# The second cross attention of a two-layer decoder follows one written table instead of rules by step

## What is computed

```python
q = x @ w_q + b_q                  # x: 2048 x 256
k = context @ w_k + b_k            # context: 1601 x 192
v = context @ w_v + b_v
q, k, v = (t.reshape(B, -1, 16, 16) for t in (q, k, v))      # 16 heads of 16
weights = softmax(einsum('bqhd,bkhd->bhqk', q, k) / 4, axis=-1)
out = einsum('bhqk,bkhd->bqhd', weights, v).reshape(B, Lq, 256)
x = layernorm(x + out @ w_o + b_o)
```

## Time and profile before

| | us |
|---|---|
| median of three executions (lowest, highest) | 3368.96 (3361.8, 3370.19) |
| the profiled execution's own time | 3361.29 |
| its span on the core | 3359.5 |
| first scores of unit 0 to the last values of unit 15 | 2530.6 to 3154.1 |

### The profile page before, as it was taken

The page is one execution under the profiler, slowest core; times in us unless marked ns, Lnnn a source line. Parts: engine busy times, 40 slices in busy tenths (PEclk is TensorE's granted clock), DMA queues, the critical chain, the costliest instruction groups (busy, mean ns, idle before and its releaser), DMA issues. The chain is left out here.

```text
span 3359.5 us, 62575 instructions
## 1 busy us (share of the span) xinstructions
PE 3055.7 (91%) x24201; PEld 1779.1 (53%) x24201; DVE 2373.0 (71%) x4987; ACT 1697.8 (51%) x2102; POOL 1735.9 (52%) x1163
## 2 busy tenths in 40 slices
PE   7999999989999999999999827779989999999797
PEld 3666666654555555555555406646654434444346
DVE  5999999945676666776667382175448979888418
ACT  3888888843444444444444322222325756666641
POOL 5999999924878788787888802223440000000002
PEclk9999999989999999999999958979988999999898
DMA  2000000020000000000000076610021201210101
GB/s 69 9 2 2 2 2 2 27 55 3 4 1 4 1 4 4 1 4 1 4 1 1 1 236 195 168 41 1 1 45 18 28 9 23 28 21 2 34 1 38
DMA packets 65530, 91.51 MB, mean 27 GB/s; under 512 B 9586, under 2 KB 55539, under 8 KB 64371
## 3 DMA queue, kind: packets, MB, share of 16 engines
q1 hardware_dynamic: 61682, 83.17, 9.8%
q0 software_dynamic: 3072, 4.34, 0.7%
q10 hardware_dynamic: 512, 0.26, 0.0%
HBM read 62.34 MB, written 10.65 MB: 22 GB/s over the span
## 5 line engine op out<-in xcount | busy, mean ns | idle before, releaser
L980 DVE TENSOR_REDUCE x0hm<-x0pM 128x1 f32<-128x400 f32 (+1 forms) x1024 | 536.6, 568 | 211.8 <-PE x0pM L884 203.5
L434 POOL TENSOR_SCALAR rows<-rows,mb 128x1024 bf16<-128x1024 bf16 x512 | 568.0, 1121 | 96.5 <-DVE mb L382 96.5
L376 DVE TENSOR_SCALAR_CACHE_REDUCE rows<-pS 128x1024 bf16<-128x1024 f32 x512 | 605.6, 1208 | 2.0 <-PE pS L312 1.5
L445 ACT ACTIVATE prT<-pP 128x1024 bf16<-128x1024 bf16 x512 | 522.3, 1024 | 109.9 <-PE pP L323 92.4
L1445 DVE TENSOR_REDUCE x1hm<-x1pM 128x1 f32<-128x400 f32 (+1 forms) x1024 | 518.9, 566 | 67.5 <-PE x1pM L1331 64.1
L1564 ACT ACTIVATE x1pr<-x1pST 128x1024 f32<-128x1024 f32 (+1 forms) x416 | 403.9, 1022 | 216.1 <-PE x1pST L1383 216.0
L844 POOL TENSOR_TENSOR x0acc<-x0acc,o_nat 128x1024 f32<-128x1024 f32 (+1 forms) x176 | 422.1, 2398 | 84.7 <-ACT o_nat L1091 64.9
L844 POOL TENSOR_TENSOR x0acc<-x0acc,x0pr 128x1024 f32<-128x1024 f32 (+1 forms) x176 | 421.7, 2396 | 83.7 <-ACT x0pr L1091 61.6
L2678 POOL MEMSET f_tri<- 128x128 f32 x1 | 0.2, 209 | 676.2 <-POOLq L1236 676.2
L1331 PE MATMUL x1pM<-x1sk,x1sq 64*128 64x400 f32 (+1 forms) x1024 | 321.9, 443 | 15.0 <-DVE x1ql L1436 4.1
L1091 ACT ACTIVATE x0pr<-x0pST 128x1024 f32<-128x1024 f32 (+1 forms) x208 | 211.9, 1027 | 234.3 <-PE x0pST L928 230.4
(11 more groups left out here) (367 smaller groups left out, 5072.1 us busy)
## 6 DMA issues: line engine op xcount, KB each, us to landing
m_w<-in_moe_w1T SPq DMA_DIRECT2D x16, 1024.0 KB, 11.4
m_w<-in_moe_w2T SPq DMA_DIRECT2D x16, 1024.0 KB, 8.4
acc_d<-m_zero SPq DMA_DIRECT2D x8, 514.0 KB, 8.2
m_acc<-acc_d SPq DMA_DIRECT2D x8, 514.0 KB, 5.6
x1sq<-x1qh SPq DMA_DIRECT2D x32, 128.0 KB, 4.0
x1sk<-x1kh SPq DMA_DIRECT2D x32, 100.1 KB, 3.6
rows_d<-m_xr SPq DMA_DIRECT2D x1, 2176.0 KB, 7.8
g_xN<-in_x SPq DMA_DIRECT2D x1, 2048.0 KB, 8.4
```

The source lines that it names most:

```text
L376: nc.vector.tensor_scalar(rows[u][:, half * 1024:(half + 1) * 1024], pS[half][:, :], 1.0, None, ALU.mult, ALU.max, accum_out=mx[u][:, half ...
L434: nc.gpsimd.tensor_scalar(r, r, -1.0, mb[u][:, 0:1], ALU.mult, ALU.add).then_inc(s_df, 1)
L445: nc.scalar.activation(prT[u][:, half * 8:(half + 1) * 8, :], pP[half][:, :, :], ACT.Exp, scale=-1.0 / HD ** 0.5).then_inc(s_ex, 1)
L980: emptied(nc.vector.tensor_reduce(hm[g % 2][:, a, t, i % 8 // 2:i % 8 // 2 + 1], bank(name)[:, 0:w], AX.X, ALU.max, negate=True), name)
```

## The change

The rules go. A table of words, `ORDER`, gives the order of one unit: `M` the next piece, `S3b` the second scores of step 3, `V3x` and `V3y` the halves of the values of step 3 (`V-1` is the last step of the unit before), `copy`, `norm`, and `unit0` to `unit4`, places for the other work. `order_of(u)` turns it into names, and TensorE, VectorE and ScalarE all follow that list. What stood at `unit0` and `unit1` goes behind `norm`. So the four projections of unit 4, and those of unit 5, stand in a row behind the norm, and a turn with its two outs does so in units 9 to 12. The names, the tiles, the instructions and the waits are the same as before.

```diff
-    def units_in(u, kt):
-
-        whole = []
-        if u == 4 and kt >= 6 and kt % 2 == 0:
-            whole.append(("q", 1, kt // 2 - 3))
...
-        return parts[:2], parts[2:4], whole, parts[4:]
...
+    ORDER = (
+        "M unit0 M S0a S0b M V-1x M M V-1y M M copy S1a S1b M V0x M M V0y M M V1x M S2a M unit1 norm "
+        "unit2 unit3 S2b M unit4 M V1y S3a unit5 M S3b M M V2x M S4a M V2y M S4b M M V3x S5a M M V3y M "
...
+    def whole_unit(u, i):
+
+        if u == 4 and i < 4:
+            return [("q", 1, i)]
+        if u == 5 and i < 4:
+            return [("k", 1, i)]
+        if 9 <= u < 13 and i < 3:
+            return [("turn", 0, u - 9) if i == 0 else ("out", 0, u - 9, i - 1)]
+        if u == HALVES - 1:
+            c, i = i // 3, i % 3
+            return [("turn", 1, c) if i == 0 else ("out", 1, c, i - 1)] + [("stats", c)] * (i == 2)
+        return []
+
+    def order_of(u):
+
+        names, late, i = [], [], MX * (u + 1) + AHEAD
+        normed = u == 0
+        for word in ORDER:
+            if word[0] == "S":
+                names.append(("scores", u, int(word[1:-1]), "ab".index(word[-1])))
+            elif word[0] == "V" and u * STEPS + int(word[1:-1]) >= 0:
+                names.append(("values", u * STEPS + int(word[1:-1]), "xy".index(word[-1])))
+            elif word == "M":
...
+            elif word[:4] == "unit":
+                if normed:
+                    names += whole_unit(u, int(word[4:]))
+                else:
+                    late += whole_unit(u, int(word[4:]))
+        return names
...
-                    for kt in range(STEPS):
-                        front, middle, whole, rest = units_in(u, kt)
-                        scores(u, kt, 0)
-                        for name in front:
-                            unit(name)
-                        scores(u, kt, 1)
-                        if u or kt:
-                            values(u * STEPS + kt - 1, 0)
-                        for name in middle:
-                            unit(name)
-                        if u or kt:
-                            values(u * STEPS + kt - 1, 1)
-                        for name in whole + rest:
-                            unit(name)
+                    for name in order_of(u):
+                        if name[0] == "scores":
+                            scores(name[1], name[2], name[3])
+                        elif name[0] == "values":
+                            values(name[1], name[2])
+                        elif name in number:
+                            unit(name)
```

More of the change, by code:

```diff
@@ L1161, in units_of @@
-    def units_of(u, kt):
-        return [name for names in units_in(u, kt) for name in names]
+    ORDER = (
[4 rows of a table added]
+        "M M S12b M V11y").split()
+    def whole_unit(u, i):
[9 more added lines that the diff above has]
+        return []
@@ new lines, in order_of @@
+    def order_of(u):
[7 more added lines that the diff above has]
+            elif word == "M":
+                if i < HALVES * MX:
+                    names.append(("max", i))
+                if i % MX == 5 and i > MX and i // MX <= HALVES:
+                    names.append(("shift", i // MX - 1))
+                i += 1
+            elif word == "norm" and u >= 1:
+                names += [("norm", u - 1)] + late
+                normed = True
+            elif word == "copy" and u >= 1:
+                names.append(("copy", u - 1))
+            elif word[:4] == "unit":
[4 more added lines that the diff above has]
+        return names
@@ L1168, in l1_cross_heads @@
     first_maxima = []
-    for i in range(done(-1, 0)):
+    for i in range(MX + AHEAD):
         first_maxima.append(("max", i))
@@ L1172, in l1_cross_heads @@
             first_maxima.append(("shift", 0))
[L1173 to L1176, removed]
+    for name in first + first_maxima + [n for u in range(HALVES) for n in order_of(u)] + last:
+        if name[0] not in ("scores", "values", "copy", "stats"):
+            number[name] = count
+            count += 1
     with ExitStack() as ctx:
@@ L1520, in _ @@
                 for u in range(HALVES):
-                    for kt in range(STEPS):
-                        for name in units_of(u, kt):
+                    for name in order_of(u):
+                        if name[0] == "stats":
+                            statistics(name[1])
+                        else:
                             unit(name)
-                        if u == HALVES - 1 and kt in (8, 11):
-                            statistics(kt // 11)
                 norm(last[0])
@@ L1596, in _ @@
                 for u in range(HALVES):
[L1597 to L1606, removed]
+                    for name in order_of(u):
+                        if name[0] == "scores":
+                            exponentials(name[1], name[2], name[3])
+                        elif name[0] == "copy":
+                            copy_out(name[1])
+                        elif name[0] in ("q", "k"):
+                            high(name)
+                        elif name[0] == "turn":
+                            turned_rows(name)
                 copy_out(HALVES - 1)
```

## The result

The changed kernel takes 3323.3 us as a median (3318.69 to 3325.58, four executions) against 3365.9 for the kernel before; the ratio is 0.9876 (95% interval 0.9863 to 0.9889). The forecast was 3336, in a range of 3322 to 3356: faster, and near the lower end of the range. The profiled execution went from 3361.3 to 3322.6, and of these 38.7 us the stretch from the first scores to the last values gives 37.3 (2530.2 to 3116.4 instead of 2530.6 to 3154.1).

A forecast was written before the change was run, and what follows sets the result against it. Neither TensorE nor VectorE was full; each waited for the other once a step, over a piece's bank. Order -32, projections -4, last unit +3 gave -33 from 3361.3, so 3328; median 7.7 higher, 3336 us, range 3322 to 3356.

The forecast's parts named there:

- The plain step: Five-piece step: second scores no longer stand behind the piece waiting for its bank; 2.78 to 2.58 us, saving 0.20.
- Rival 2: Plain step: the wait moves to the third piece, directly before the values, and half the gain goes; 3352 us, chance 0.19.
- rival 4: Blocks: more pieces stand alone ahead of scores or values and hold them up; slower, 3384 us, chance 0.08.
- ScalarE makes values wait: Sign that the forecast is wrong: values on TensorE held up by ScalarE; no size given.
- The unit: Order within units: 2.2 us saved in each of units 1 to 14 and 1.3 in unit 0, together -32.
- The joint of values in steps 10 and 11: Second values of step 10 joined to first of step 11: 1.00 us against 2 x 0.57, gain 0.1 a unit.
- The term for the maxima's row: First scores of a unit wait 0.41 us for the maxima's row; the table shifts it earlier, gain 0.4 a unit.
- rival 3: VectorE's reductions bound the kernel, so the order changes nothing; 3361 to 3376 us, chance 0.07.
- The projections: Units 4 and 5, projections in a row: -10.6 saved, +3.5 idle, +3.0 half clock; -4 us, between -10 and +2.
- The wait for the stack and the clock behind it: Unit 4: TensorE idles 3.5 us before the fourth q projection, then a half-clock stretch costs 3.0.
- The last unit: Unit 15: norm, turns and outs ahead of step 2's second scores leave ScalarE without work; +3 us, between 0 and +5.
- rival 1: The plain step gains as counted; 3336 us, own range 3324 to 3348, chance 0.66.

The follow-up runs named there:

- e1: The kernel before with one edit: in every step the second piece moves from before the second scores to behind them; 3324.7 us, ratio 0.9889.
- e5: The changed kernel with six table blocks of three pieces and two scores put back to second scores last, directly before the values; 3343.3 us, ratio 0.9947.
- f4: The changed kernel with unit 15 in old order, unit 4's q projections later, and the joined pair of values taken apart by a piece; 3313.6 us, ratio 0.9862.
- e7: The changed kernel with unit 15 in old order, q projections later, and reductions reading only half their columns (not a usable kernel); 3291.3 us, ratio 0.9799.
- e3: The changed kernel with unit 4's four q projections still side by side but behind the values of step 5; 3317.3 us, ratio 0.9869.
- e2: The changed kernel with unit 15 in the old order (norm, turns and outs a step apart, behind both halves of the values); 3313.1 us, ratio 0.9857.
- f2: The changed kernel with unit 15 in the old order, measured again on one chip beside the changed kernel; 3313.8 us, ratio 0.9861.
- e6: The changed kernel with both repairs: unit 15 in the old order and unit 4's q projections behind the values of step 5; 3314.5 us, ratio 0.9862.
- f3: Both repairs (unit 15 in old order, q projections later) on the changed kernel, measured again on one chip beside it; 3310.1 us, ratio 0.9853.
- e4: The changed kernel's table with the eight projections of units 4 and 5 one by one, two steps apart, at the old places; 3324.3 us, ratio 0.9889.

## Why the prediction was right, and where a size was off

**The plain step.** The mechanism was right: the last piece of a block waits for its bank (the second of the pair), and what stands behind it waits too. 2.58 was forecast, 2.56 came; e1 makes it with one swap, e5 unmakes it. Inside the block two errors cancel, and that is luck. The second scores were counted at 0.34, with the middle piece, and start at 0.52. The third piece was counted at 0.64 to 0.68 and starts at 0.78, not for its bank (its weight load follows that of the scores without a wait) but behind the scores. In turn it was given 0.38 to the values and takes 0.27, so the values come at 1.05 where 1.02 to 1.06 was counted. Rival 2 (the wait moves before the values) and rival 4 (lone pieces hold up others) are refuted by this, and by the plain units.

**A sign that did come.** "ScalarE makes values wait" was to show the forecast wrong. The weight loads for values do wait for an exponential now, 156 times, where they did 21 times before:

```profile
PEld x1pO L1398 <- ACT x1pr L1564: 4.0, 21, 0.2
PEld x1pO L1408 <- ACT x1pr L1567: 33.8, 156, 1.2
```

But these are waits of loads, 150 of them outside unit 15 and there at most 0.4 us long, while TensorE is busy for 34.26 of the 34.30 us of a plain unit. The matmuls of values wait for ScalarE only twice, 1.2 us in all, both in unit 15, and in the plain step they follow the piece in 0.27. The sign was too coarse as it was written.

**The unit.** -32 was forecast for the order, and -39.6 came: 2.7 a plain unit instead of 2.2. Two terms were too small. The steps were put at 2.0 (ten of them, 0.20 each); in e1 eleven steps are each 0.22 shorter, 2.4. The joint of values in steps 10 and 11 was put at 0.1, and f4 gives 0.4. The reckoning compared 1.00 with twice 0.57 alone and left out the 0.38 from the piece between them to the next values, while the piece itself finds a place in another block. (That is read from the rows; f4 shows the 0.4, not its parts.) The term for the maxima's row was put at 0.4: from the last piece to the first scores of a unit it is 0.36 us before and 0.10 after, as means of units 1 to 14, so about 0.3. Taken together this is 3.1, and 2.7 was measured. So the blocks with two scores in a row, put at a loss of 0.3, seem to cost 0.4; that is an estimate, for the terms come from two different orders and need not add up.

That the old order waits for the transfer of the row shows in the weight loads for scores: in the kernel before, in e1, where faster steps leave the transfer less time, and in the changed kernel, where the one wait is in unit 15:

```profile
PEld x1pST L1383 <- DMA x1sq<-x1nt: 2.5, 9, 0.6
PEld x1pST L1383 <- DMA x1sq<-x1nt: 6.7, 14, 1.7
```

```profile
PEld x1pST L1393 <- DMA x1sq<-x1nt: 0.7, 1, 0.7
```

**VectorE as the bound (rival 3).** It was not before, or the order alone could not have given 2.7 us a unit with the same reductions; and e7 shows that it is not now, but for 0.8 us a unit.

**The projections.** -4 was forecast and -4.7 came (units 4 and 5 stand 18.7 over plain ones instead of 23.4). The two halves of this sum were off in opposite directions, so that it came out so near is luck. A projection in a row was put at 1.71, which no run shows; three of them take 5.42, 1.8 each. With neither wait nor half clock (unit 4 of e3, unit 5) the eight stand 14.7 over plain units and not 12.8, so standing side by side saves 8.7 and not 10.6. The wait for the stack and the clock behind it were put at 3.5 and 3.0, 6.5 together; e3 takes both away for 4.0 (46.4 to 42.4), the idle time was 2.5, and the half clock cost the fourth projection 1.7. Both were right in kind.

**The last unit.** +3 was forecast, between 0 and +5, and +7.0 came. The mis-sized term is the hole between the two scores of step 2. It was put at 4.4, the lengths of what stands in it; in e3, at full clock, it is 5.4 from the norm to the second scores (3082.54 to 3087.90). Two waits within it, 0.97 and 0.78, were put at nothing; without them it would be 3.6. With this the row costs the 4.4 of e3 instead of 3; how the rest of that divides was not tried. The stretch at half clock, 2.6 more, was not in the sum either, though one had been priced for unit 4.

**The sum.** -39.6 - 4.7 + 7.0 = -37.3 in the stretch, where -33 was forecast; 1.4 more lie outside it, in parts of the program that the change does not touch. The median lies 12.7 under the forecast of 3336, and the larger part of that has nothing to do with the order: 4.3 come from the stretch, 1.4 from outside, and 7.0 from the last step of the sum, which put the median 7.7 above the profiled execution because it was so in three executions before. In the changed kernel it lies 0.7 above. So 3323.3 is inside the stated range by 1.3 us, and just under the own range of rival 1 (3324 to 3348), whose mechanism is the one that was shown.

## What to carry to other kernels

In an engine that takes its instructions in order, look at what stands behind each instruction that waits. Here one matmul that waited 0.3 us for a bank held up scores that had all they needed; to put it behind them gave 33 of the 37 us that a large rewrite gave. A row of like work, side by side, saves the waits between its pieces, but it should stand where its inputs have landed and where no other engine lives from the work behind it. When such a row is priced, the waits within it count as well as its matmuls, and a fall of TensorE's clock may come on top.

## What the runs showed of the hardware

- A half of the values costs 0.57 us where pieces follow and 1.00 for two halves in a run. The Trainium skill (TensorEngine Tiling, Key Properties) states that a change of tiling mode drains TensorE; these times fit with that. Taking the one joined pair of a unit apart cost 0.4 us (f4), but f4 also moves a piece, so this is the price of the move and not of the change of mode alone.
- The granted clock fell to half behind 2.5 us of idle TensorE in unit 4, in all five traces with that wait (the changed kernel twice, e2, e5, f2), and in unit 4 of none of those with the projections later (e3, e6, f3, f4). A projection ran 3.65 us at half and 1.98 at full clock.
- In unit 15 of the changed kernel it fell too, in both traces, where TensorE's idle times ahead of it are only 0.67 and 0.96 us; in e3, e4 and e5 the same order of unit 15 kept the full clock, and in e1 the old order lost it, behind 1.18 us. Why one order kept its clock in some programs and lost it in others was not settled.
